# A fused two-layer block on one Trainium2 core: in the second attention, the score products of four heads issued together

## What is computed

```python
q = _ln((x @ Wq + bq).reshape(b, s1, H, HD), qn_w, qn_b)
kv = concatenate([y_main @ Wk + bk, y_main @ Wv + bv], axis=-1).reshape(b, s2, H, 2 * HD)
k = _ln(kv[..., :HD], kn_w, kn_b); v = kv[..., HD:]
k_dca = _ln((y_dca @ Wkv_dca + bkv_dca)...[keys]); v_dca = ...[values]
ctx     = softmax(q @ k.T * HD ** -0.5) @ v            # 240 keys
ctx_dca = softmax(q @ k_dca.T * HD ** -0.5) @ v_dca    # the other 16 keys
x = x + tanh(g_xattn[1]) * ((ctx + ctx_dca) @ Wo + bo)
```

## Time and profile before

| | us |
|---|---|
| median of three runs | 3731.29 |
| lowest, highest | 3731.02, 3732.23 |
| the profiled execution, whole time | 3731.69 |
| its span, first to last instruction | 3729.9 |
| from the first scores of the second attention to those of pair 126 | 675.1 |

### The profile page before, as it was taken

One profiled execution on the slowest core, in us unless ns is written; L12 is line 12 of the kernel. 1 busy time (PEld: TensorE's weight loads), 2 busy tenths in 40 slices (PEclk: granted clock), 3 DMA queues, 4 the chain that ended last, 5 costly groups with the idle time before them and its releaser, 6 DMA issues. The chain is left out here.

```text
span 3729.9 us, 68005 instructions
## 1 busy us (share of the span) xinstructions
PE 3581.6 (96%) x23268; PEld 3103.4 (83%) x23268; DVE 2182.2 (59%) x5411; ACT 1822.4 (49%) x4698; POOL 1531.7 (41%) x1536
## 2 busy tenths in 40 slices
PE   7999999999999998699999997999999899999999
PEld 7999999999999997699999985666666578877777
DVE  6666666556666665566666676777777542222221
ACT  4444445544444443455555544777777632222222
POOL 3333333534444443465566644766666430000000
PEclk9999999999999999899999998999999899999999
DMA  4566665316666661666666652221221120000000
GB/s 153 177 224 222 228 224 214 126 57 218 217 217 217 217 224 51 234 240 227 239 233 240 231 189 94 67 64 60 65 64 61 40 82 23 23 23 23 23 23 23
DMA packets 227766, 520.16 MB, mean 139 GB/s; under 512 B 12273, under 2 KB 28914, under 8 KB 223474
## 3 DMA queue, kind: packets, MB, share of 16 engines
q1 hardware_dynamic: 122866, 296.36, 22.8%
q10 hardware_dynamic: 94432, 187.71, 13.6%
q0 software_dynamic: 10272, 33.63, 2.7%
HBM read 266.52 MB, written 251.13 MB: 139 GB/s over the span
## 5 line engine op out<-in xcount | busy, mean ns | idle before, releaser
L672 POOL TENSOR_SCALAR a_prob<-a_prob,a_rinv 128x256 f32<-128x256 f32 x512 | 471.3, 931 | 836.0 <-DVE a_rinv L855 836.0
L619 ACT ACTIVATE a_prob<-a_prob,a_low_bias 128x256 f32<-128x256 f32 x512 | 256.5, 502 | 458.6 <-DVE a_low_bias L846 458.6
L1118 PE MATMUL e_gb<-e_xt_hi,in_hi 128*128 128x256 f32 x1248 | 354.5, 284 | 5.7 <-DVE e_xt_lo L1244 5.7
L1120 PE MATMUL e_gb<-e_xt_hi,in_lo 128*128 128x256 f32 x1248 | 354.4, 284 | 0.0
L1102 POOL TENSOR_TENSOR e_act_hi<-e_act_f,e_zeros 128x256 fp32r<-128x256 f32 x156 | 234.6, 1504 | 285.3 <-DVE e_act_f L1264 273.7
L1119 PE MATMUL e_gb<-e_xt_lo,in_hi 128*128 128x256 f32 x1248 | 351.5, 282 | 0.0
L2242 ACT ACTIVATE f_h_f<-f_hb,b_sb 128x512 f32<-128x512 f32 x128 | 88.1, 688 | 478.3 <-PE f_hb L2180 414.4
L422 PE MATMUL a_pj<-a_xt,a_wq_hi 128*128 128x256 f32 x1024 | 310.2, 303 | 0.9 <-DVE a_q_lo L705 0.9
L424 PE MATMUL a_pj<-a_xt,a_wq_lo 128*128 128x256 f32 x1024 | 289.4, 283 | 0.0
L423 PE MATMUL a_pj<-a_xt,a_wq_hi 128*128 128x256 f32 x1024 | 289.0, 282 | 0.0
L705 DVE TENSOR_TENSOR a_ot_lo<-a_avb,a_ot_hi 128x256 fp32r<-128x256 f32 x256 | 108.3, 423 | 254.4 <-ACT a_ot_hi L624 254.4
(11 more groups left out here) (362 smaller groups left out, 11370.7 us busy)
## 6 DMA issues: line engine op xcount, KB each, us to landing
raw_in<-in_w_gate SPq DMA_DIRECT2D x39, 2048.0 KB, 7.8
x_sorted<-a_blank ACTq DMA_DIRECT2D x42, 1792.0 KB, 6.5
y_sorted<-a_blank ACTq DMA_DIRECT2D x42, 1792.0 KB, 8.5
raw_out<-in_w_out SPq DMA_DIRECT2D x39, 1024.0 KB, 5.1
e_xg<-x_sorted SPq DMA_DIRECT2D x39, 512.0 KB, 8.4
y_sorted<-e_y_sb SPq DMA_DIRECT2D x39, 512.0 KB, 2.8
xt_rows<-a_xt SPq DMA_DIRECT2D x16, 1024.0 KB, 5.1
a_xt<-xt_rows SPq DMA_DIRECT2D x16, 1024.0 KB, 5.2
```

Source lines behind the costliest of these rows:

```text
L619: e = nc.scalar.activation(prob[:, u % 4, t], prob[:, u % 4, t], ACT.Exp, bias=low_bias[:, u % 2, t:t + 1], scale=-1.0, accum_out=rsum[:, ...
L672: p = nc.gpsimd.tensor_scalar(prob[:, u % 4, t], prob[:, u % 4, t], rinv[:, u % 2, t:t + 1], None, ALU.mult)
L1118: nc.tensor.matmul(out, a_hi, b_hi, start=start, stop=False)
L1120: return nc.tensor.matmul(out, a_lo, b_hi, start=False, stop=stop)
```

## The change

Scores are issued for a whole group, in odd steps only. In step u = 2g - 1 PE computes all four heads of group g: eight instructions, the loop over the heads inside the one over the two query tiles, so that four row parts of the array and four banks follow each other. They wait until the exponentials of all pairs up to 2g - 1 are done (before: of all but the latest), since all four banks are written. The place in the step moves from its start to behind `turn_qk`, ahead of the second head's `turn_p`.

On ACT `exps` is no longer split by head. In an odd step it stands whole at the start, ahead of both `copy_pt`; in an even step it stands behind the first head's `copy_pt` and `ot_hi`. DVE gets a wait on `t_ready` for odd pairs: the buffer `prob` of four pairs is written again, and the order of PE's work no longer says by itself that its old content has been transposed.

```diff
-            def scores(i, n):
-                g, first = divmod(n, 2)
-                if first == 0:
-                    pe.wait_ge(taken["qk"], 2 * GROUPS * i + g + 1)
-                pe.wait_ge(e_done, LOOP * i + n + 1)
+            def scores(i, g):
+                pe.wait_ge(taken["qk"], 2 * GROUPS * i + g + 1)
+                pe.wait_ge(e_done, LOOP * i + 2 * g + 2)
                 for t in range(2):
-                    for j in range(2):
-                        at = (2 * first + j) * HD
-                        mm = nc.tensor.matmul(sc[:, n % 2, j, t * S:(t + 1) * S], qk[at:at + HD, g % 2, t * P:(t + 1) * P],
+                    for h in range(HG):
+                        at = h * HD
+                        mm = nc.tensor.matmul(sc[:, h // 2, h % 2, t * S:(t + 1) * S], qk[at:at + HD, g % 2, t * P:(t + 1) * P],
                                               qk[at:at + HD, g % 2, S:], start=True, stop=True)
-                mm.then_inc(s_ready, 1)
+                mm.then_inc(s_ready, 2)
...
-                if pair(i, u + 1):
-                    scores(i, u + 1)
...
                 for bb, g in due(i, u, "qk"):
                     turn_qk(i, bb, g)
+                if u % 2 and pair(i, u + 1):
+                    scores(i, (u + 1) // 2)
                 if pair(i, u - 2):
                     turn_p(i, u - 2, 1)
...
+                if u % 2 and pair(i, u):
+                    exps(i, u)
+                if pair(i, u - 2):
+                    copy_pt(i, u - 2, 0)
+                if u % 2 == 0 and pair(i, u - 4):
+                    g = (u - 4) // 2
+                    act.wait_ge(av_ready, 2 * GROUPS * i + g + 1)
+                    nc.scalar.copy(ot_hi[:, g // GROUPS % 2, g % GROUPS], avb[:, 0:S]).then_inc(ot_hid, 1)
+                if u % 2 == 0 and pair(i, u):
+                    exps(i, u)
+                for bb, g in due(i, u, "qk"):
...
+                if pair(i, u - 2):
+                    copy_pt(i, u - 2, 1)
...
                     dve.wait_ge(s_max, N + 1)
+                    if N > 3 and n % 2:
+                        dve.wait_ge(t_ready, 2 * (N - 3))
```

More of the change, by code:

```diff
@@ L1757, in turned_ahead, with exps @@
                 nc.scalar.copy(ahead.xt_hi[:, c], sc[:, c // 2, c % 2]).then_inc(ff_xt_hid, 1)
-            def exps(i, n, j):
+            def exps(i, n):
                 p, s = prob[:, n % 4], sc[:, n % 2]
-                if j == 0:
-                    act.wait_ge(s_bias, LOOP * i + n + 1)
-                    nc.scalar.activation(p[:, :, :, 0:DCA], p[:, :, :, 0:DCA], ACT.Exp).then_inc(d_done, 1)
-                for t in range(2):
-                    e = nc.scalar.activation(p[:, j, t, DCA:], s[:, j, t * S + DCA:(t + 1) * S], ACT.Exp, bias=nmax[:, n % 2, 1, 2 * j + t:2 * j + t + 1],
-                                             accum_out=rsum[:, n % 4, 1, 2 * j + t:2 * j + t + 1])
-                if j == 1:
-                    e.then_inc(e_done, 1)
+                act.wait_ge(s_bias, LOOP * i + n + 1)
+                nc.scalar.activation(p[:, :, :, 0:DCA], p[:, :, :, 0:DCA], ACT.Exp).then_inc(d_done, 1)
+                for j in range(2):
+                    for t in range(2):
+                        e = nc.scalar.activation(p[:, j, t, DCA:], s[:, j, t * S + DCA:(t + 1) * S], ACT.Exp, bias=nmax[:, n % 2, 1, 2 * j + t:2 * j + t + 1],
+                                                 accum_out=rsum[:, n % 4, 1, 2 * j + t:2 * j + t + 1])
+                e.then_inc(e_done, 1)
             def copy_pt(i, n, j):
@@ L1784, in step @@
                     nc.scalar.activation(sq[:], nrm[:, bb % 2, 2 * half:2 * half + 2], ACT.Square).then_inc(sq_done, 1)
-                for j in range(2):
-                    if pair(i, u):
-                        exps(i, u, j)
-                    if j == 1:
-                        for bb, g in due(i, u, "qk"):
-                            act.wait_ge(ready["qk"], GROUPS * (2 * i + bb) + g + 1)
-                            of = room(f"qk{g}")
-                            for n, cols in enumerate((slice(0, S), slice(S, S + DCA), slice(S + DCA, 2 * S))):
-                                l = nc.scalar.activation(qk[:, g % 2, cols], of[:, cols], ACT.Identity, bias=ln_sb[:, 2 * n + 1:2 * n + 2], scale=ln_sb[:, 2 * n:2 * n + 1])
-                            l.then_inc(taken["qk"], 1)
-                    if pair(i, u - 2):
-                        copy_pt(i, u - 2, j)
-                    if j == 0 and u % 2 == 0 and pair(i, u - 4):
-                        g = (u - 4) // 2
-                        act.wait_ge(av_ready, 2 * GROUPS * i + g + 1)
-                        nc.scalar.copy(ot_hi[:, g // GROUPS % 2, g % GROUPS], avb[:, 0:S]).then_inc(ot_hid, 1)
+                if u % 2 and pair(i, u):
[9 more added lines that the diff above has]
+                for bb, g in due(i, u, "qk"):
+                    act.wait_ge(ready["qk"], GROUPS * (2 * i + bb) + g + 1)
+                    of = room(f"qk{g}")
+                    for n, cols in enumerate((slice(0, S), slice(S, S + DCA), slice(S + DCA, 2 * S))):
+                        l = nc.scalar.activation(qk[:, g % 2, cols], of[:, cols], ACT.Identity, bias=ln_sb[:, 2 * n + 1:2 * n + 2], scale=ln_sb[:, 2 * n:2 * n + 1])
+                    l.then_inc(taken["qk"], 1)
+                if pair(i, u - 2):
+                    copy_pt(i, u - 2, 1)
                 for bb, in due(i, u, "turn"):
```

## The result

The changed kernel takes **3799.6 us** (median of 4 runs, 3797.0 to 3804.7) against 3731.2 us (4 runs, 3729.6 to 3732.2) for the kernel before on the same chip: 1.0185 times as long, 95% interval 1.0168 to 1.0203. It is slower by 68 us; the forecast was 3779, in a range of 3745 to 3825. The profiled execution has a span of 3798.1 us, that of before 3729.9, so 68.2 us have to be found.

A forecast was written before the change was run, and what follows sets the result against it. PE was taken to bound the kernel before, and a ring through PE and ACT after. 3731.7 + 32 (rings) - 5 (ends) + 20 (clock falls) = 3779 us, range 3745 to 3825, inner range 3765 to 3800.

The forecast's parts named there:

- The bound: Steady sequences: PE bounds them at 42.4 us each; its own work falls by 4.6 us, from 40.8 to 36.2.
- The block: PE's scores of four heads: 1.06 us, as four row parts run side by side; upper end 2.12 us.
- The ring: Block to next block through PE and ACT: 44.7 us a sequence against 42.4 before, +32 us over 14 sequences.
- from step 7: Group starting in step 7: `turn_x` waits until DVE has taken k1, making 11.85 us from block to block.
- from step 1: Group starting in step 1: ACT's square needs q1 taken, 4.97 instead of 4.74, so 11.3 us from block to block.
- from step 3: Group starting in step 3: no late unit, but values wait for the second head's copy; 10.46 us from block to block.
- from step 5: Group starting in step 5: PE and ACT work and hand-overs from block to block sum to about 11.1 us.
- The clock: PE in the steady part: 8 falls to 1.2 GHz in 14 sequences, +20 us, between none and 20 falls (+50).
- The ends: First and last sequences: -3 in the last, -1 at the beginning, -1 behind the last pair; -5 us, between -9 and +3.
- PE stays the bound: Rival for the steady part: rings under 9.45 us, so the saving is kept; 3662 us, chance 0.07.
- Not side by side: Rival for PE's score block: four parts don't run together, the block costs 2.1 us; 3846 us, chance 0.10.
- No fall: Rival for PE's clock: it never falls in the steady part; 3759 us, 3745 to 3765, chance 0.21.

The follow-up runs named there:

- experiment 5: The changed kernel with ACT's exponentials first in every step, ahead of the square and the copies: 3768.7 us, ratio 1.0098.
- experiment 7: The changed kernel with ACT's exponentials first in every step and unit k1 taken ahead of the maxima on DVE: 3754.0 us, ratio 1.0059.
- the filler, experiment 8: The changed kernel with ten unread matmuls 128x256 on PE in step 7, ahead of the first head's transposes: 3786.4 us, ratio 1.0146.
- experiment 12: The kernel of experiment 10 with `turn_qk` issued ahead of unit k0 on PE in step 6: 3719.5 us, ratio 0.9968.
- experiment 10: The changed kernel with exponentials first and the square behind first copy and `ot_hi` on ACT, k1 and o0 taken earlier on DVE: 3720.6 us, ratio 0.9971.
- experiment 11: The kernel of experiment 10 with PE's scores put back to a pair of heads in every step: 3721.3 us, ratio 0.9973.
- experiment 1: The changed kernel with each block's score instructions issued as two halves, row parts 0 and 1 first, then 2 and 3: 3802.6 us, ratio 1.0192.

## Why the prediction was right, and where it was off

**The bound, right.** "PE is the bound there": with 96% busy in 42.4 us it was, and most of the saving of 4.6 us of its work for a sequence is there. PE's busy time fell from 40.8 to 37.65 us. Each wait also lets a tail count as busy (four transposes last 0.60 to 0.66 where the next instruction starts 0.41 after them, if it needn't wait), some 0.2; there are 7 waits in a clean sequence after and 3 in one before. Without the tails it is about 40.2 and 36.2, an estimate, and the saving about 4.0. The forecast reached 36.2 by two errors that cancel: its 40.8 had tails in it, and its 4.6 left out that the values, which stood behind scores before, now cost 0.1 more on the way in, as its own ring has it (2346.96 to 2347.29, 0.33 us where 0.23 is usual).

**The block, right.** 1.08 us against 1.06 taken. The Trainium skill, "TensorE: Matmul & The Clock Gate", gives four row parts 3.07 times the rate, by which it was to be 1.38; the trace has 16 records in about the time of 8 on two parts, so here nothing is lost from two parts to four.

**The ring, right, and short by about 0.95 us a sequence.** Clean rings, forecast and measured: from step 7 11.85 and 12.09, from step 1 11.3 and 11.42, from step 3 10.46 and 10.88, from step 5 11.11 and 11.28. Together 44.7 and 45.67, which makes +45.5 us instead of +32. The mis-sized terms:
- The hand-over from ACT's copy to PE's transposes, taken as 0.05, is 0.15 (copy ended 2375.70, transposes 2375.85), and the copy lasts 0.63 behind the scaling where 0.59 was taken. Both stood in the rows: 2641.35 + 0.58 is 2641.93, and PE began at 2642.07; 2644.09 lasted 0.63. With the block's 0.02 that is 0.15 in each ring, 0.6 a sequence, 8.4 us in all, missed although my own rows had it. A further 0.09 in the ring from step 7 I can't assign.
- In the ring from step 3 unit o1 waits 0.25 us for DVE's taking of o0, a member that the ring didn't have. PE's transposes start at 2364.30 and the unit at 2364.93 instead of 2364.68. It became the largest wait of experiments 5 and 7 (1.57 us).
- The sum for step 1, given as 4.97, is 4.92; the ring of 11.3 holds with either.

**DVE's new wait and the queues of POOL and SP, right.** No row of the waits after has DVE waiting for PE's transposes there, and POOL still has 409 us in 654.

**The clock, right in kind and nearly in size.** 9 falls for 8, 1.6 us each for 2.5, 14.4 us for 20. The price came from a fall in the first sequence whose stretch at half clock was 6.6 us long. The one shown here lasts about 3.4 us, with PE busy all through; half of that is 1.7, an estimate that fits the 1.6. So a longer fall was taken as the price of a short one. What the engine did ahead of the fall shown was 0.99 us of work in 3.3 us, with one gap of 2.31; such a gap stands in 13 of the 14 sequences, 9 of which had a fall behind it, and with the filler that broke it up there was none. The Trainium skill, same page, "Why this matters for your kernels", ties the fall to one unbroken idle gap longer than that, by which there would have been none; the measurement decides against it here.

**The ends, wrong.** -5 us were taken and +8.2 came. "There the unit k1 now comes first and fills that": it did come first, but PE waited 1.29 us for its bank and then did it at the lowered clock, and the first scores, behind it, are 3.3 us later. The first sequence was put at "about 43" by the steady rings; it is 46.9 with a clock of 0.89, and its last ring alone is 13.33. Where the clock is down (0.66 in the last sequence, 0.68 before) the steady rings' lengths don't hold. For the last sequence the prediction had this: with PE's part doubled it came to about 39, and 39.6 was measured; but then it took 3 us less than the 37.6 of before, between that and the 31.4 of full clock. Taken together the sum has errors of +13.5 (rings), -5.6 (clock), +13.2 (ends), 21 us in all, which is the difference between 3779 and 3800. That the time lies just within the inner range of 3765 to 3800 says little: by its own terms (no fall to 15 falls, the rings off by 0.2 each) that range would be some 3748 to 3807.

**The rivals.** "PE stays the bound": its condition, a ring under 9.45 us, is met nowhere in the steady part, not even in experiment 12 (10.1 to 11.0). "The orders of ACT and PE leave no such shortcut" is right for this kernel only: experiment 10 shortens all four rings by 0.7 to 1.4 us with the same instructions in another order. "Not side by side" is out by the block's 1.08 us. "No fall" would have been 3786 by the filler, not 3759, since the rings and the ends were put too short.

**What stays open.** Why exactly these sequences of the 14 have a fall and the others not; and whether the block is worth anything once the orders fit (experiment 11).

## What to carry to other kernels

Making the bound engine's work shorter gains only as far as the next ring allows. Before merging two steps into one, write out what the merged step now waits for, and the way from its end back to its start through every engine; compare the sum with the bound engine's own work. Then look at each member for work that merely stands in its way in the queue: here four moves on ACT and DVE gave 79 us back, and once they were made, the kernel with and without the merged step took the same time.

## What the runs showed of the hardware

- Matmuls on other row parts run beside earlier ones even when they are queued behind all of them: 16 records take 1.09 us in two halves (experiment 1) and 1.08 us with the parts interleaved (the kernel after), and their starts spread over 0.8 us in both.
- Unread matmuls in a gap can shorten a kernel: ten of them, 1.45 us of PE's time in each sequence, took 13 us away, by keeping the clock up (experiment 8).
- DVE's short operations on the roots (128x64) are mostly 0.20 to 0.22 us, and some are 1.01 us with the same shape, in the trace of experiment 7 for example these two; POOL was multiplying from 2359.19 to 2361.12, during the first, and stood still from there to 2363.77, during the second, but no run tested that this is the cause.

```profile
2360.19 1.01 DVE L1520 SCALAR_TENSOR_TENSOR d_hrstd<-d_hroot,d_hrstd 128x64 f32<-128x64 f32 x1
...
2363.05 0.20 DVE L1520 SCALAR_TENSOR_TENSOR d_hrstd<-d_hroot,d_hrstd 128x64 f32<-128x64 f32 x1
```
